# Two half-width transfers of a B or C row become one full-width transfer with a two-row source, in a selective-scan kernel on one core

## What is computed

```
def step(h, inp):
    u_t, d_t, b_t, c_t = inp
    dA = jnp.exp(d_t[..., None] * A)
    h = dA * h + (d_t * u_t)[..., None] * b_t[:, :, None, :]
    y = jnp.einsum('bkdn,bkn->bkd', h, c_t)
    return (h, y)
```

## Time and profile before

| What | Value |
|---|---|
| Median of 3 runs | 12109.58 us (12099.88 to 12118.07) |
| The profiled execution's own time | 12101.1 us |
| Its span, first to last instruction | 12099.2 us |
| PE, DVE, ACT, POOL busy | 88%, 87%, 77%, 79% of the span |
| Mean granted TensorE clock | 0.967 |
| Moved by DMA | 2207.14 MB, mean 182 GB/s |

### The profile page before, as it was taken

The page is one execution under the profiler, slowest core; times in us unless marked ns, Lnnn a source line. Parts: engine busy times, 40 slices in busy tenths (PEclk is TensorE's granted clock), DMA queues, the critical chain, the costliest instruction groups (busy, mean ns, idle before and its releaser), DMA issues. The chain is left out here.

```text
span 12099.2 us, 124903 instructions
## 1 busy us (share of the span) xinstructions
PE 10610.6 (88%) x35606; PEld 4918.4 (41%) x35606; DVE 10566.9 (87%) x7439; ACT 9359.5 (77%) x20340; POOL 9502.9 (79%) x4213
## 2 busy tenths in 40 slices
PE   7988889898898988989889898898988988889888
PEld 3444334443344433444334443344433444334443
DVE  6999779996799977999679996799967999689996
ACT  5888678885788867888578885788867888678885
POOL 4999459994599945999459994599945999369993
PEclk9999989999999999999999999999998999999999
DMA  4687447774477744777447774477744777447773
GB/s 136 225 225 223 116 129 225 224 220 112 132 225 223 222 108 140 223 223 221 104 143 222 223 223 99 145 224 221 222 100 144 226 225 219 98 151 224 225 222 90
DMA packets 678831, 2207.14 MB, mean 182 GB/s; under 512 B 165153, under 2 KB 167201, under 8 KB 666721
## 3 DMA queue, kind: packets, MB, share of 16 engines
q1 hardware_dynamic: 678144, 2199.17, 62.8%
HBM read 2101.48 MB, written 67.44 MB: 179 GB/s over the span
## 5 line engine op out<-in xcount | busy, mean ns | idle before, releaser
L1339 POOL TENSOR_TENSOR state<-state,c_sb 128x1024 f32<-128x1024 f32 x3072 | 7175.5, 2369 | 230.2 <-DMA c_sb<-bc 127.7
L1089 PE MATMUL ps<-state,wt 128*128 128x512 f32 x12288 | 5736.9, 600 | 67.1 <-ACT ya L1160 26.1
L1307 DVE TENSOR_TENSOR_SCAN state<-decay,carry,ps 128x1024 f32<-128x1024 f32 x1728 | 3988.0, 2338 | 40.7 <-issue 5.7
L1089 PEld LDWEIGHTS ps<-state,wt 128*128 128x128 f32 x12288 | 2262.9, 191 | 2256.8 <-issue 1931.2
L1213 ACT ACTIVATE dbu_t<-du_t,b_t 128x128 f32<-128x128 f32 (+1 forms) x10176 | 2951.1, 366 | 25.3 <-PE ps L1080 25.3
L1232 ACT ACTIVATE decay<-delta,a_neg 128x1024 f32<-128x1024 f32 x2304 | 2641.0, 1146 | 0.1
L1328 POOL TENSOR_TENSOR dbu<-b_sb,du 128x1024 f32<-128x1024 f32 x768 | 1814.2, 2362 | 175.2 <-DVE du L1312 152.8
L1294 DVE TENSOR_TENSOR ps<-ps,du 128x1024 f32<-128x1024 f32 x1288 | 1555.1, 1207 | 40.0 <-PE ps L1034 40.0
L1167 ACT COPY carry<-state 128x1 f32<-128x1 f32 x3072 | 568.5, 185 | 1273.4 <-DVE state L1307 1258.4
L1034 PE MATMUL ps<-parts,sel 114*128 114x512 bf16 (+1 forms) x2576 | 793.1, 390 | 794.7 <-DVE state L1307 792.9
L1307 DVE TENSOR_TENSOR_SCAN state<-ps,carry,dbu 128x1024 f32<-128x1024 f32 x576 | 1347.9, 2340 | 130.2 <-POOL dbu L1328 108.1
(11 more groups left out here) (218 smaller groups left out, 10031.8 us busy)
## 6 DMA issues: line engine op xcount, KB each, us to landing
c_sb<-bc SPq DMA_DIRECT2D x2048, 512.0 KB, 4.6
c_sb<-bc SPq DMA_DIRECT2D x2048, 256.0 KB, 5.9
b_sb<-bc SPq DMA_DIRECT2D x512, 512.0 KB, 4.0
b_sb<-bc SPq DMA_DIRECT2D x512, 256.0 KB, 4.0
x_nat<-x SPq DMA_DIRECT2D x17, 1536.0 KB, 14.6
gates<-gate_a SPq DMA_DIRECT2D x8, 2048.0 KB, 6.8
x_tok<-x SPq DMA_DIRECT2D x288, 48.0 KB, 1.9
gn<-gn_t SPq DMA_DIRECT2D x8, 1536.0 KB, 7.1
```

Of the source, the lines that this page charges most:

```text
L1089: mm = pe.matmul(py[:, q * CH:(q + 1) * CH], col("ident"), state[:, slot(g, n), q * CH:(q + 1) * CH], start=(n == 0), stop=False)
L1307: dve.tensor_tensor_scan(state[:, slot(g, n), way], rate, what, 0.0 if fresh else carry[:, n:n + 1], ALU.mult, ALU.add)\
L1339: pool.tensor_tensor(state[:, slot(g, n), :], state[:, slot(g, n), :], c_sb[:, n % CRING, :], ALU.mult).then_inc(S["weighted"], 1)
```

## The change

For the passes over two halves, the pair of transfers is replaced by one whose destination is all 128 lanes. Its source is written as two rows (one for each direction), each repeated 64 times. The counts that POOL waits for go down to 16 for a row everywhere, since there is one transfer for each row.

```
-            def c_landed(T, c, n):
-
-                before = sum(32 if t % 3 == 2 else 16 for t in range(T)) * (NSC * NS // CRING)
-                return (c * (NS // CRING) + (n // CRING + 1)) * (32 if T % 3 == 2 else 16) + before
+            def c_landed(g, n):
+
+                return 16 * (g * (NS // CRING) + n // CRING + 1)
...
-                return sum((32 if h // NSC % 3 == 2 else 16) for h, m in order_of[:g * NS + n + 1]
-                           if made(h, m) == BY_POOL)
+                return 16 * so_far(BY_POOL, g, n)
...
                         if T % 3 < 2:
-                            sp.dma_start(dst, bc_dram[2 * (T // 3) + kind, T % 3, n:n + 1, span(at * SC, SC)]
-                                         .broadcast_to([128, SC])).then_inc(S[landed], 16)
+                            row = bc_dram[2 * (T // 3) + kind, T % 3, n:n + 1, span(at * SC, SC)].broadcast_to([128, SC])
                         else:
-                            for h in range(2):
-                                sp.dma_start(dst[DR * h:DR * h + DR, :],
-                                             bc_dram[2 * (T // 3) + kind, h, n:n + 1, span(at * SC, SC)]
-                                             .broadcast_to([DR, SC])).then_inc(S[landed], 16)
+                            row = bc_dram[2 * (T // 3) + kind, :, n, span(at * SC, SC)].unsqueeze(1)\
+                                .broadcast_to([2, DR, SC])
+                        sp.dma_start(dst, row).then_inc(S[landed], 16)
```

More of the change, by code:

```diff
@@ L1337, in steps @@
                             pool.wait_ge(S["carried"], g * NS + n + 1 + CREDIT)
-                            pool.wait_ge(S[f"c_in_{n % CRING}"], c_landed(T, c, n))
+                            pool.wait_ge(S[f"c_in_{n % CRING}"], c_landed(g, n))
                             pool.tensor_tensor(state[:, slot(g, n), :], state[:, slot(g, n), :], c_sb[:, n % CRING, :],
```

## The result

The changed kernel takes 21,787.64 us (median, 21,779.78 to 21,787.94) against 12,111.17 us for the kernel before in the same session. The ratio is 1.7989, with a 95% interval of 1.7969 to 1.8009. The forecast was 22,008 us, 1.0% too high, and the range 21,350 to 24,800 us.

A forecast was written before the change was run, and what follows sets the result against it. POOL was taken to bound every pass; with two engines each pass gains 819.2 + 2.5 + 2.4 - 12.5 - 193.0 = 618.6 us, sixteen passes 9,898 us, giving 22,008 us. The range was 21,350 to 24,800 us.

The forecast's parts named there:

- POOL sets the pace of every pass of the kernel before: Every pass before the change: POOL's 80 products of 2.32 us fill it, with DVE just behind.
- Two engines for each row: New transfers in passes over two halves: the source's outermost count of 2 confines each to two DMA engines; 84%.
- The rival that the destination's 128 lanes decide: New transfers: 16 engines share each row and the 108.5 us of waits go, giving 12,001 us; chance 9%.
- The rule that the prediction quotes: DMA transfers: engine count is the largest number up to 16 dividing the slowest dimension of both sides.
- The port rule: SBUF writes: 64 lanes reach 8 of 16 ports, all 128 reach 16; two half transfers don't make up for it.
- A piece of 0.160 us: New transfers: each 4 KB piece takes an engine 0.160 us, so a row of 64 pieces takes 10.24 us.
- The term of 819.2 us a pass: Each pass over two halves: 80 rows at 10.24 us of transfer on the two engines.
- The ends of a pass: Each of 16 passes: add 2.5 us start-up and 2.4 us last product, less 12.5 us issued ahead.
- Latency and B rows hidden: Changed passes: four C buffers keep 30 us of work queued, so the two engines, also carrying B, never run dry.
- the forecast of 40 us: Changed passes: a C row lands about 40 us after issue, since four queue up.
- SP costs nothing: SP's issues: 80 instead of 160 transfers a pass save some 0.6 us each, worth 0 since SP waits for POOL.
- TensorE's clock: TensorE, idle four fifths of the changed passes, may get a lower clock: 3.2 us after each, some 50 us, inside the range.

The follow-up runs named there:

- the runs with 4, 8 and 64 outermost: Changed kernel, its source in the passes over two halves given four rows, eight rows or 64 repeats as outermost dimension: 15,424.43, 12,926.52 and 11,984.15 us.
- the spread halves: Kernel before, pairs of 64-lane transfers kept, but the first written to even lanes and the second to odd ones: 11,984.05 us, ratio 0.9906.
- The run with B alone: Changed kernel, with the new transfer for rows of B only and rows of C fetched by pairs again: 15,068.07 us.
- 16 source rows of 8 lanes each: Changed kernel, source of 16 rows each repeated for 8 lanes: 12,072.31 us with right rows copied within DRAM, 12,031.07 us without copies (wrong rows).
- 32 rows of 4 lanes: Changed kernel, source of 32 rows each repeated for 4 lanes: 11,977.30 us without copies (wrong rows), 12,079.81 us with copies bunched, 11,984.37 us with smaller copies spread.

## Why the prediction was right

**POOL sets the pace of every pass of the kernel before.** Confirmed: pass 3, which was not touched, still has POOL busy for all of its 185.4 us. In pass 2 POOL's work is unchanged at 187 us, and the two engines set the pace, as forecast.

**Two engines for each row.** Right. Two closing packets a row show it, and the runs with 4, 8 and 64 outermost put the cause at the source's outermost count. The rival that the destination's 128 lanes decide is refuted by the same runs, since the destination never changed. The rule that the prediction quotes from the Trainium skill ("DMA: Bandwidth & Descriptors", section "Why a DMA increments its semaphore by 16 and not by 1") gives this count. It held at every source count tried: 2, 4, 8, 16, 32 and 64. The destination's count was always 128. The port rule that it quotes from the Trainium skill ("SBUF — State Buffer", section "Door 1: The DMA port swizzle") has full-width transfers reach all ports. It agrees with the pair's 0.271 us and with 0.200 us once each half is spread over all lanes, but it is not enough: full width from 16 rows took 0.27 to 0.28 us. That two half transfers don't make up for one was seen here for neighbouring lanes; the spread halves ran as fast as one transfer.

**A piece of 0.160 us.** Slightly too high; the low end of the range had allowed for pieces that overlap a little. The records show 0.160 us of busy time for a piece (0.128 x 16 x 600 / 7,683), but pieces follow each other every 9.98 / 64 = 0.156 us: they overlap by a few nanoseconds. The term of 819.2 us a pass was in truth 798.4, and 16 passes make 333 us of that. This is more than the whole miss of 213 us in the profiled execution (21,999 against 21,786).

**The ends of a pass.** Too low by what remains, 333 - 213 = 120 us or 7.5 us a pass. I had counted start-up and one product, and taken off the 12.5 us by which the first row is issued ahead. In the first image that head start was given back: the early row held up the last row of pass 1, which took 12.4 us longer. Rows of the 128-lane passes before and after also share the two engines: eight pieces each, 1.25 us. At the end of pass 2, POOL's products lie 10.6 to 12.0 us apart. This part of the sum I only read from the timeline and did not test by a run. That the time came within 1.0% owes something to luck, since the two errors have opposite signs.

**Latency and B rows hidden.** Right for the kernel as changed: the share of 2.05 engines leaves no gap. The profile gives no landing time for these rows, so the forecast of 40 us stays open. The run with B alone shows the condition under which it fails.

**SP costs nothing.** Right in effect, but not in the way that I gave. I bounded an issue by 1.9 us. Issues took up to 17.5 us, because SP itself was held, and that changed nothing as the two engines had work.

**TensorE's clock.** The granted clock went to 0.62 in pass 2, so it spent most of the pass at 1.2 GHz, the lower of its two levels; PE was busy for only 284 of the 788.7 us. Its work there had taken 170 us before, and the longer work is all beside the transfers. Pass 3 was back at 0.99 and no longer than before, so the 50 us that I allowed for didn't come.

## What to carry to other kernels

Before merging transfers, look at the outermost count of the source as well as that of the destination; the runs here changed only the source's. A source of two rows puts a 512 KB transfer on two engines, and the number of closing packets tells how many take part. Two transfers of 64 neighbouring lanes cost less than that by far. Where a wide transfer needs different rows for different lanes, give it enough source rows of constant distance (here 32, by copies within DRAM), and spread the copying over stretches in which the DMA engines have time.

## What the hardware showed that I had not expected

**16 engines are not enough.** With 16 source rows of 8 lanes each a piece took 0.27 to 0.28 us, with 32 rows of 4 lanes or 64 pairs 0.20 us. The trace doesn't name an engine's lanes. One reading, not shown: with 16 rows each engine is tied to 8 neighbouring lanes, and two engines meet at one SBUF port. The Trainium skill, "DMA: Bandwidth & Descriptors", section "The descriptor swizzle", has an engine write two groups of four lanes that lie 32 apart, both by one port, in a plain full-width transfer. That fits the faster shapes, if the one with 32 rows is split the same way. But with four rows, if each engine takes one row's 32 lanes, lanes 32 apart belong to different engines too, and a piece took 0.161 us. So the reading doesn't fit all runs as it stands. For the pairs a run changed the destination's lanes and nothing else (0.271 and 0.200 us). For the 16 rows no run separates the destination from the source.

**Contention can change within a pass.** Four engines kept 0.161 us a piece (0.259 x 16 x 360 / 9,264). Eight had 0.188 us on average, but not evenly. This is what they moved in forty slices of 5 us, from 600 to 800 us:

```profile
GB/s 147 151 154 154 152 152 156 157 159 197 168 141 152 193 210 210 172 164 202 152 158 181 185 193 210 165 199 206 169 163 186 164 183 194 160 195 206 209 213 194
```

The same kind of transfer starts the stretch at about 150 GB/s and ends it above 200. As an argument only: engines that start in step collide, and drift apart with time. With the 16-row source the share is still 0.91 and 0.94 on average over 160 us.

**SP is held in the issue.** In pass 2 an issue took 9.78 us, the pace of the transfers themselves:

```profile
566.42 0.60 SPq L984 DMA_DIRECT2D b_sb<-bc  x1
567.07 20.58 SPq L984 DMA_DIRECT2D c_sb<-bc  x4
587.69 9.78 SPq L984 DMA_DIRECT2D b_sb<-bc  x1
```

The issue of B at 587.69 had no semaphore left to wait for: the B product before it ran from 583.14 to 585.48 us. So with a few such transfers pending, the next instruction of SP waited inside the issue, and everything behind it on SP waited too. In this kernel nothing else was behind it.
